# Decoder kernel, state-space stage: scans issued in pairs, once per two groups

## The chip, the cores and the metric

One core of one Trainium2 chip runs the whole program. The metric is the device time of one execution in microseconds; lower is better. The engines are TensorE (PE; its weight loads are listed apart as PEld), VectorE (DVE), ScalarE (ACT), GpSimd (POOL) and SyncE (SP), each with a queue of its own that it works through in order.

## What is computed

Six blocks with residual additions over x of 4 x 256 tokens of 256 elements: self-attention, an expert layer chosen by token number, a mixture of experts, a state-space block (stage D of the kernel), an attention over given keys and values (stage E), and another mixture of experts (stage F). The change touches only the state-space block. Its core is this, for each batch and chunk of 128 tokens:

```python
Lm = jnp.exp(segsum(A))                       # 64 heads x 128 x 128, zero above the diagonal
Y_diag = jnp.einsum('bcshn,bczhn,bhcsz,bczhp->bcshp', Cm, Bm, Lm, X)
states = jnp.einsum('bcshn,bhcs,bcshp->bchpn', Bm, decay_states, X)
...
Y_off = jnp.einsum('bcshn,bchpn,bhcs->bcshp', Cm, states, state_decay_out)
return (Y_diag + Y_off).reshape(b, l, h, p)
```

## The kernel before

A planner, `schedule`, writes one list of steps, and every engine walks through the same list and issues its own part of each step, so the list sets the order on each queue. Between engines stand semaphores.

In stage D the work is cut into 8 units (4 batches x 2 chunks of 128 tokens), numbered u = 0 to 7, and each unit into 16 groups of 4 heads, numbered hg = 0 to 15. Over all units the groups are k = 16u + hg, 0 to 127. A step `("ssd", "D", (u, hg))` does for its group k:

- PE: two bf16 matmuls of 512 columns into one bank of a ring of three (`a_bank`): the mask of later tokens (line 1450), then the decay exponents (line 1452), which has 15 rows of contraction. Then `scan` of group k - 3 (`LAG = 3`, line 95).
- ACT: the exponential from that bank into tile M[k % 4] (line 1055). Before it, ACT waits until the scan of group k - 4 has read that tile.
- DVE: M[k % 4] times the products C·B of the group (line 1807), in place.

`scan` (line 1114) is four fp32 matmuls, one per head, each with a stationary tile of 32 columns of its own and 128 columns of M. Each shows in the trace as two MATMUL rows, so one scan is 8. It waits for the multiplication on DVE of the same group. The four write the four quarters of the partitions of one bank, O; four groups in a row accumulate into one block of 128 columns of it.

Behind each `ssd` step the planner places other work of the stage (`beside`): projections of a later batch (`din`: PE line 1391, then ACT lines 983 and 985, DVE line 1749, ACT line 996, DVE line 1759) at groups 1, 4 and 9 of units 0 to 4; of the next unit: `at` (PE 1418) at group 6, `dz` (PE 1397) at 8, `zs` (ACT, DVE 1767) at 10, `xt` (PE 1428) at 12, `cb` (PE 1437, DVE 1797) at 13; of the last unit: `y_t` at 3 (ACT line 1066 copies the finished bank O, PE line 1260 turns it, DVE lines 1833 to 1839 finish it), `dy_t` (PE 1484, ACT 1071) at 5 and `dy` (PE 1490) at 7; of this unit, at group 0, `state` (PE 1466 in even units, PE 1476 and DVE 1816 in odd ones). After units 2, 4 and 6 DVE also normalises a batch for stage E. Within a step, PE issues the two decay matmuls, then the scan, then the work beside it.

Of the kernel before, what the change touches and what calls it, by code (L numbers as in the profile page):

```python
# [78 lines left out]
NHG = NV // HG  # L79
# [15 lines left out]
LAG = 3  # L95
# [272 lines left out]
def decoder(nc, A, out, stages="ABCDEF"):  # L368
    steps = schedule(stages)
    at = number(steps)  # L370
    with ExitStack() as ctx:
# [702 lines left out]
        def _(pe):  # L1074
# [27 lines left out]
            def scan(s, u, hg):  # L1102

                k = NHG * u + hg
                if hg == 0:
                    bk = o_bank("ssd", s, u)

                    pe.wait_ge(xsp_ready, u + 1)
                pe.wait_ge(m_ready, k + 1)
                bk = O[at["O"]["ssd", s, u] % 2]  # L1110
                quarter, h = divmod(hg, HG)
                for j in range(HG):

                    ins = mm(bk[j * 32:(j + 1) * 32, quarter * P:(quarter + 1) * P],  # L1114
                             xsp[u % 2][:, quarter, h, j, :, :].rearrange("p q w -> p (q w)"),
                             M[:, k % NM, j * P:(j + 1) * P], start=(h == 0), stop=(h == HG - 1), skip_group_check=True)
                ins.then_inc(m_used, 1)

            pe.wait_ge(const_in, 64)
            for kind, s, i in steps:  # L1120
# [28 lines left out]
                elif kind == "qkv_mm" and s == "A":  # L1149
                    i, t = i  # L1150
# [42 lines left out]
                elif kind == "m_t":  # L1193
                    k = attn_index(s, i)
# [6 lines left out]
                elif kind == "pv":  # L1201
                    i, step = i
# [177 lines left out]
                elif kind == "din":  # L1380
                    b, j = i
                    if PAIRS * b + j < beside_c:
                        pe.wait_ge(mix_in, 96)
                        bk, full = t_bank("din", s, b, j), t_full
                    else:
                        bk, full = a_bank("din", s, b, j), a_full
                    pe.wait_ge(t_read, at["T"]["lt", s, b] + 1)
                    for h in range(2):
                        ct = 2 * j + h
                        for k in range(KD):  # L1390
                            ins = mm(bk[:, h * L:(h + 1) * L], win[:, k, ct * P:(ct + 1) * P],  # L1391
                                     xnT_of(s)[:, k, b * L:(b + 1) * L], start=(k == 0), stop=(k == KD - 1))
                    ins.then_inc(full, 1)
                elif kind == "dz":
                    bk = v_bank("dz", s, i)
                    for k in range(KD):
                        ins = mm(bk[:, :], xnT_of(s)[:, k, i * P:(i + 1) * P], win[:, k, CONV:CONV + DI],  # L1397
                                 start=(k == 0), stop=(k == KD - 1))
                    ins.then_inc(v_full, 1)
                elif kind == "dt_in":  # L1400
                    bk = t_bank("dt_in", s, i)
                    pe.wait_ge(t_read, at["T"]["lt", s, B - 1] + 1)
                    for u in range(NU):
                        for k in range(KD):
                            ins = mm(bk[:, u * NV:(u + 1) * NV], xnT_of(s)[:, k, u * P:(u + 1) * P],
                                     win[:, k, CONV + DI:], start=(k == 0), stop=(k == KD - 1))
                    ins.then_inc(t_full, 1)
                elif kind == "acum":

                    pe.wait_ge(dt_ready, 1)  # L1410
                    for k in range(2):
                        bk = t_bank("acum", s, k)
                        mm(bk[:, :], tri[:, k, :], t_max, start=True, stop=True).then_inc(t_full, 1)
                elif kind == "at":
                    bk = t_bank("at", s, i)
                    pe.wait_ge(ap_ready, 1)
                    for h in range(2):
                        ins = tr(bk[:, :].bitcast(BF16)[0:RA, h * P:(h + 1) * P],
                                 ap_[:, i, 2 * h:2 * h + 2, :, :].rearrange("p j m g -> p (j m g)"), identb[:, :])
                    ins.then_inc(t_full, 1)  # L1420
                elif kind == "xt":
                    b, c = divmod(i, NT)

                    pe.wait_ge(xs_ready, (CT // 2) * (b + 1))
                    for part in range(2 if c == 0 else 1):
                        bk = a_bank("xt", s, i, part)
                        for k in range(4):
                            ins = tr(bk[:, k * P:(k + 1) * P], xs[:, b % 2, 4 * part + k, c * P:(c + 1) * P], ident[:, :])
                        ins.then_inc(a_full, 1)
                elif kind == "cb":  # L1430
                    b, c = divmod(i, NT)

                    banks = [v_bank("cb", s, i, par) for par in range(2)]
                    for g2_ in range(NG // 2):
                        for par in range(2):
                            rows = slice(NS * par, NS * par + NS)
                            ins = mm(banks[par][:, g2_ * P:(g2_ + 1) * P], xs[rows, b % 2, 4 + g2_, c * P:(c + 1) * P],
                                     xs[rows, b % 2, 8 + g2_, c * P:(c + 1) * P], start=True, stop=True)
                            if g2_ == NG // 2 - 1:
                                ins.then_inc(v_full, 1)  # L1440
                elif kind == "ssd":
                    u, hg = i
                    if hg == 0:

                        if u == 0:
                            pe.wait_ge(hot_in, 64)
                        pe.wait_ge(rows_landed, 16 * 6 * (u + 1))
                    bk = a_bank("ssd", s, u, hg)

                    mm(bk[:, :], identb[:, :], maskt[:, :].unsqueeze(1).to_broadcast([P, HG, P]),  # L1450
                       start=True, stop=False, skip_group_check=True)
                    mm(bk[:, :], rows_z[u % 2][:, hg, :], rows_s[u % 2][:, :, hg, :], start=False, stop=True,  # L1452
                       skip_group_check=True).then_inc(a_full, 1)
                    k = NHG * u + hg - LAG
                    if k >= 0:
                        scan(s, *divmod(k, NHG))
                elif kind == "ssd_end":
                    for k in range(NHG * i - LAG, NHG * i):
                        scan(s, *divmod(k, NHG))
                elif kind == "state" and i % 2 == 0:  # L1460
                    bk = t_bank("state", s, i)
                    pe.wait_ge(xd_ready, i // 2 + 1)
                    pe.wait_ge(a_read, at["A"]["xt", s, i, 1] + 1)
                    for g_ in range(NG):
                        lo = NS * (g_ % 2)
                        ins = mm(bk[lo:lo + NS, (g_ // 2) * NS:(g_ // 2 + 1) * NS], Bt[:, g_ * NS:(g_ + 1) * NS],
                                 XD[:, g_ * NS:(g_ + 1) * NS], start=True, stop=True)
                    ins.then_inc(t_full, 1)
                elif kind == "state":
                    b = i // NT  # L1470
                    pe.wait_ge(t_read, at["T"]["state", s, i - 1] + 1)
                    banks = [v_bank("state", s, i, par) for par in range(2)]
                    for g2_ in range(NG // 2):
                        for par in range(2):
                            rows = slice(NS * par, NS * par + NS)
                            ins = mm(banks[par][:, g2_ * NS:(g2_ + 1) * NS], xs[rows, b % 2, 8 + g2_, P:L],
                                     stt[rows, g2_, :], start=True, stop=True)
                            if g2_ == NG // 2 - 1:
                                ins.then_inc(v_full, 1)
                elif kind == "dy_t":  # L1480
                    bk = t_bank("dy_t", s, i)
                    pe.wait_ge(yf_ready, i + 1)
                    for k in range(DI // P):
                        ins = tr(bk[:, k * P:(k + 1) * P], yf[:, k * P:(k + 1) * P], ident[:, :])
                    ins.then_inc(t_full, 1)
                elif kind == "dy":
                    bk = v_bank("dy", s, i)
                    pe.wait_ge(t_read, at["T"]["dy_t", s, i] + 1)
                    for k in range(DI // P):
                        ins = mm(bk[:, 0:D], yfT[:, k, :], wout[:, k, :], start=(k == 0), stop=(k == DI // P - 1))  # L1490
                    ins.then_inc(v_full, 1)
# [434 lines left out]
```

## Time and profile before

| what | value |
|---|---|
| median of 3 runs | 1000.64 us |
| lowest and highest | 997.29 and 1004.06 us |
| span of the profiled execution | 1004.2 us |
| of it, state-space groups (first decay matmul to last scan) | about 461 to 713 us |
| PE busy over the span | 822.1 us (82%) |
| DVE busy over the span | 584.5 us (58%) |

The span is counted from the first to the last instruction of the profiled execution. No separate time was taken for that execution; its span lies at the upper end of the three runs. In the rows, times are microseconds from the start of the span. "idle before <-X" in brackets is how long the engine stood idle before that row and what released it.

### The profile page before, as it was taken

How to read it: one execution, taken by the hardware profiler on the slowest of the kernel's cores; microseconds unless marked ns; L12 is line 12 of the kernel's file. 1: busy time of each engine (PE TensorE's matmuls, PEld its weight loads, DVE VectorE, ACT ScalarE, POOL GpSimd, SP SyncE). 2: the span in 40 equal slices, each digit the busy share in tenths (PEclk: the TensorE clock that was granted, in tenths of full speed). 3: DMA queues.
4: the chain of work that ended last, by engine and by line, in shares of the span. 5: the costliest groups of instructions: out<-in, count | busy, mean ns of one | idle time of the engine just before them, and what ended most of it. 6: DMA issues, size and time to landing. Idle time of an engine off the chain costs nothing.

```text
span 1004.2 us, 14716 instructions
## 1 busy us (share of the span) xinstructions
PE 822.1 (82%) x5680; PEld 530.7 (53%) x5680; DVE 584.5 (58%) x1184; ACT 380.8 (38%) x653; POOL 221.1 (22%) x210
## 2 busy tenths in 40 slices
PE   1678777599899799657899899999757777899998
PEld 0334443258677588523444444434434554677776
DVE  5765642544545457535787878547577663645443
ACT  1124334001444356244455445335213345444442
POOL 3200000123433322041110111001231111432432
PEclk9989878599899899866999999669578799799999
DMA  8000001000121211100000000000000001232231
GB/s 307 28 2 1 3 1 48 1 0 23 57 79 55 72 48 32 18 0 5 5 6 5 4 3 5 5 5 2 1 2 2 2 2 49 64 93 64 79 92 45
DMA packets 17669, 32.98 MB, mean 33 GB/s; under 512 B 5642, under 2 KB 9610, under 8 KB 17320
## 3 DMA queue, kind: packets, MB, share of 16 engines
q1 hardware_dynamic: 17600, 32.03, 10.4%
q8 instruction: 46, 0.75, 0.3%
q14 instruction: 23, 0.19, 0.1%
HBM read 30.06 MB, written 1.05 MB: 31 GB/s over the span
## 4 chain that ended last, share of the span: by engine, by line
PE 57%; DVE 21%; issue 11%; ACT 5%; POOL 4%; DMA 1%; SPq 0%; DVEq 0%; ACTq 0%; POOLq 0%
PE bank L1352 12%; PE bank L1376 8%; PE bank L1391 5%; PE bank L1299 3%; PE bank L1114 3%; PE bank L1452 2%; DVE s_arena L1807 2%; DVE s_xn L1523 2%; PE bank L1490 2%; PE bank L1314 2%; PE bank L1450 2%; DVE s_arena L1749 2%; PE bank L1243 2%; DVE s_arena L1595 2%; PE bank L1397 2%
## 5 line engine op out<-in xcount | busy, mean ns | idle before, releaser
L777 POOL TENSOR_TENSOR s_wl<-s_wmoe,s_wh 128x768 fp32r<-128x768 f32 x54 | 99.3, 1841 | 174.2 <-ACT s_wh L947 174.2
L1807 DVE TENSOR_TENSOR s_arena<-s_arena 128x512 f32<-128x512 f32 x128 | 89.8, 711 | 54.9 <-ACT s_arena L1055 54.5
L1055 ACT ACTIVATE s_arena<-bank 128x512 f32<-128x512 f32 x128 | 74.6, 602 | 74.8 <-PE bank L1452 74.8
L896 ACT ACTIVATE s_arena<-bank 128x512 f32<-128x512 f32 x96 | 56.6, 597 | 106.9 <-PE bank L1219 59.2
L1595 DVE TENSOR_REDUCE s_arena<-bank 128x2 f32<-128x512 f32 (+1 forms) x96 | 64.8, 687 | 35.0 <-PE bank L1190 18.6
L1714 DVE TENSOR_TENSOR s_act<-bank,s_sg_moe 128x512 f32<-128x512 f32 x54 | 37.4, 692 | 81.5 <-PE bank L1352 75.0
L1352 PE MATMUL bank<-s_xh,s_wh 128*128 128x512 f32 x216 | 73.2, 421 | 8.0 <-POOL s_wl L777 7.9
L959 ACT CAST s_ah<-s_act 128x512 fp32r<-128x512 f32 x54 | 33.6, 622 | 101.8 <-DVE s_act L1719 79.1
L1352 PE MATMUL bank<-s_xl,s_wh 128*128 128x512 f32 x216 | 69.4, 403 | 0.0
L1352 PE MATMUL bank<-s_xh,s_wl 128*128 128x512 f32 x216 | 69.2, 403 | 0.0
L1376 PE MATMUL bank<-s_wh,s_ah 128*128 128x256 f32 x216 | 66.5, 308 | 2.8 <-DVE s_al L1725 2.8
L1749 DVE SCALAR_TENSOR_TENSOR s_arena<-s_arena,s_convw 128x256 f32<-128x256 f32 x144 | 68.0, 513 | 0.6
L1376 PE MATMUL bank<-s_wl,s_ah 128*128 128x256 f32 x216 | 61.5, 285 | 0.0
L1376 PE MATMUL bank<-s_wh,s_al 128*128 128x256 f32 x216 | 61.5, 285 | 0.0
L1725 DVE TENSOR_TENSOR s_al<-s_act,s_ah 128x512 fp32r<-128x512 f32 x54 | 37.4, 692 | 40.3 <-ACT s_ah L959 40.2
L725 POOL TENSOR_TENSOR s_rstd<-s_ve,s_mhalf 128x2 f32<-128x2 f32 x24 | 16.6, 692 | 192.2 <-DVE s_ve L1515 192.1
L1450 PE MATMUL bank<-s_maskt,s_identb 128*128 128x512 bf16 x128 | 53.5, 418 | 5.5 <-issue 5.5
L1391 PE MATMUL bank<-s_xnT,s_win 128*128 128x256 f32 x192 | 53.5, 428 | 0.0
L1376 PEld LDWEIGHTS bank<-s_wh,s_ah 128*128 128x128 f32 x216 | 41.5, 192 | 13.4 <-issue 8.2
L1146 PE MATMUL bank<-s_ident,s_xn 128*128 128x128 f32 x80 | 15.7, 330 | 38.9 <-DVE s_xn L1523 36.7
L1352 PEld LDWEIGHTS bank<-s_xl,s_wh 128*128 128x128 f32 x216 | 42.3, 196 | 9.8
L1352 PEld LDWEIGHTS bank<-s_xh,s_wh 128*128 128x128 f32 x216 | 39.3, 198 | 15.5 <-DVE s_act L1714 7.0
(220 smaller groups left out, 1673.5 us busy)
## 6 DMA issues: line engine op xcount, KB each, us to landing
s_wmoe<-in_wF SPq DMA_DIRECT2D x28, 384.0 KB, 3.1
s_wmoe<-in_wC SPq DMA_DIRECT2D x26, 384.0 KB, 3.1
s_win<-in_win SPq DMA_DIRECT2D x1, 2112.0 KB, 10.5
s_x<-in_x SPq DMA_DIRECT2D x4, 256.0 KB, 3.5
s_early<-in_ctxT SPq DMA_DIRECT2D x1, 1024.0 KB, 9.5
s_ctxn<-in_ctx SPq DMA_DIRECT2D x1, 1024.0 KB, 12.4
out_x<-s_x SPq DMA_DIRECT2D x4, 256.0 KB, 2.9
s_xnT<-in_tok SPq DMA_DIRECT2D x1, 512.0 KB, 7.8
```

Source lines behind the costliest of these rows:

```text
L777: g.tensor_tensor(wl[:, w % NS_, :], wmoe[:, w % NW, :], wh[:, w % NS_, :], ALU.subtract).then_inc(wl_ready, 1)
L896: a.activation(PT[:, p % NPT, :], AR[n % 3][:, :], ACT.Exp).then_inc(a_read, 1)
L1055: a.activation(M[:, k % NM, :], AR[n % 3][:, :], ACT.Exp).then_inc(a_read, 1)
L1352: ins = mm(G[2 * (n % 2) + half][:, :], a_[:, k, half, :], b_[:, k, toks], start=(p_ == 0), stop=(p_ == len(parts) - 1))
L1376: ins = mm(Y[t // NT][:, (t % NT) * D:(t % NT + 1) * D], a_[:, w % NA, t * P:(t + 1) * P], b_[:, w % NS_, 2 * KD * P:], start=(j == 0 and ...
L1391: ins = mm(bk[:, h * L:(h + 1) * L], win[:, k, ct * P:(ct + 1) * P], xnT_of(s)[:, k, b * L:(b + 1) * L], start=(k == 0), stop=(k == KD - 1))
L1450: mm(bk[:, :], identb[:, :], maskt[:, :].unsqueeze(1).to_broadcast([P, HG, P]), start=True, stop=False, skip_group_check=True)
L1595: v.tensor_reduce(nM[:, q, h0:h0 + heads], V[n % 2][:, :].rearrange("p (h k) -> p h k", h=heads), AX.X, ALU.max, negate=True).then_inc(v_r ...
L1714: v.tensor_tensor(act_[:, w % 2, :], G[2 * (n % 2) + 1][:, :], sg_moe[:, n % 2, :], ALU.mult).then_inc(g_read, 1)
L1725: v.tensor_tensor(al[:, w % NA, :], act_[:, w % 2, :], ah[:, w % NA, :], ALU.subtract).then_inc(al_ready, 1)
L1749: ins = v.scalar_tensor_tensor(o, raw[:, m % NRAW, h, KS - 1 - k:KS - 1 - k + L], convw[:, ct, KS - 1 - k:KS - k], o, ALU.mult, ALU.add)
L1807: v.tensor_tensor(m, m, CBs[:, u % 2, hg // (NV // NG):NG:NG // HG, :], ALU.mult).then_inc(m_ready, 1)
```

## The change

PE no longer issues one scan in every group. In odd groups it issues two, of groups k - 3 and k - 2; in even groups it issues none. After the last unit two scans are left over instead of three. The order of all other instructions, the semaphores and the tiles stay as they are. The line below that reads `range(NHG * i + 1 - LAG, NHG * i)` is the rest after the last unit.

```diff
@@ -1451,11 +1451,12 @@
                        start=True, stop=False, skip_group_check=True)
                     mm(bk[:, :], rows_z[u % 2][:, hg, :], rows_s[u % 2][:, :, hg, :], start=False, stop=True,
                        skip_group_check=True).then_inc(a_full, 1)
-                    k = NHG * u + hg - LAG
-                    if k >= 0:
-                        scan(s, *divmod(k, NHG))
+                    if hg % 2:
+                        for k in range(NHG * u + hg - LAG, NHG * u + hg - LAG + 2):
+                            if k >= 0:
+                                scan(s, *divmod(k, NHG))
                 elif kind == "ssd_end":
-                    for k in range(NHG * i - LAG, NHG * i):
+                    for k in range(NHG * i + 1 - LAG, NHG * i):
                         scan(s, *divmod(k, NHG))
```

## Rows read from the trace of the kernel before

**Rows 1.** The page: busy time of each engine, and the chain that ended last
```profile
PE 822.1 (82%) x5680; PEld 530.7 (53%) x5680; DVE 584.5 (58%) x1184; ACT 380.8 (38%) x653; POOL 221.1 (22%) x210
PE 57%; DVE 21%; issue 11%; ACT 5%; POOL 4%; DMA 1%; SPq 0%; DVEq 0%; ACTq 0%; POOLq 0%
```

**Rows 2.** Busy time by stretch, the whole stage; columns in the first line
```profile
core 0: us, PE busy (x) PEld busy (x) DVE busy (x) ACT busy (x) POOL busy (x), PEclk, DMA share, GB/s
461.00:713.00 252.00, 233.66 (x1830) 112.89 (x1833) 183.00 (x356) 122.42 (x237) 30.41 (x45) 0.88 0.02 4
```

**Rows 3.** Timeline of PE, one group of unit 3: start, duration
```profile
581.50 0.39 PE L1450 MATMUL bank<-s_maskt,s_identb 128*128 128x512 bf16 x1
...
582.13 0.43 PE L1114 MATMUL bank<-s_arena,s_wmoe 128*32 128x128 f32 x8
582.49 0.39 PE L1450 MATMUL bank<-s_maskt,s_identb 128*128 128x512 bf16 x1
```

**Rows 4.** Timeline of PE in the first attention, same matmul form
```profile
95.43 0.42 PE L1243 MATMUL bank<-s_arena 128*32 128x128 f32 x8
95.79 0.66 PE L1277 MATMUL bank<-s_ident,s_arena 128*128 128x128 f32 x4
...
116.67 0.64 PE L1243 MATMUL bank<-s_arena 128*32 128x128 f32 x16
117.24 0.33 PE L1146 MATMUL bank<-s_ident,s_xn 128*128 128x128 f32 x1
...
144.91 1.08 PE L1243 MATMUL bank<-s_arena 128*32 128x128 f32 x16
145.92 0.61 PE L1186 MATMUL bank<-s_masks,s_identb 128*128 128x512 bf16 x1
```

**Rows 5.** Timeline of PE, unit 0, step 2, which has no scan
```profile
468.22 0.60 PE L1452 MATMUL bank<-s_arena 15*128 15x512 bf16 x1
468.75 0.52 PE L1450 MATMUL bank<-s_maskt,s_identb 128*128 128x512 bf16 x1
```

**Rows 6.** Timeline of PE in unit 2: `at` of the next unit
```profile
537.76 0.31 PE L1418 MATMUL bank<-s_identb,s_arena 128*96 128x128 bf16 x2 [0.20 <-ACT s_arena L1071]
```

**Rows 7.** Timeline of DVE and PE, end of unit 3
```profile
588.55 1.56 DVE L1807 TENSOR_TENSOR s_arena<-s_arena 128x512 f32<-128x512 f32 x1
590.16 0.42 PE L1114 MATMUL bank<-s_arena,s_wmoe 128*32 128x128 f32 x8 [0.97 <-DVE s_arena L1807]
```

**Rows 8.** Timeline of all engines, from unit 1 into unit 2
```profile
524.47 0.42 PE L1114 MATMUL bank<-s_arena,s_wmoe 128*32 128x128 f32 x8 [0.96 <-DVE s_arena L1807]
...
526.27 0.42 PE L1114 MATMUL bank<-s_arena,s_wmoe 128*32 128x128 f32 x8
526.63 1.99 PE L1391 MATMUL bank<-s_xnT,s_win 128*128 128x256 f32 x8
526.74 1.88 DVE L1807 TENSOR_TENSOR s_arena<-s_arena 128x512 f32<-128x512 f32 x3
...
531.01 0.61 ACT L1066 COPY s_arena<-bank 128x512 f32<-128x512 f32 x1
...
531.76 0.63 PE L1260 MATMUL bank<-s_ident,s_arena 128*128 128x128 f32 x4 [1.26 <-ACT s_arena L1066]
```

**Rows 9.** Timeline of ACT, from unit 2 into unit 3
```profile
562.83 1.02 ACT L983 ACTIVATE s_arena<-bank,s_convw 128x256 f32<-128x256 f32 x2 [3.84 <-DVE s_arena L1816]
```

**Rows 10.** Timeline of PE and DVE, unit 5, step 3
```profile
629.06 0.65 PE L1114 MATMUL bank<-s_arena,s_wmoe 128*32 128x128 f32 x8 [0.76 <-DVE s_arena L1807]
629.64 1.11 PE L1260 MATMUL bank<-s_ident,s_arena 128*128 128x128 f32 x4
629.88 1.89 DVE L1807 TENSOR_TENSOR s_arena<-s_arena 128x512 f32<-128x512 f32 x3
```

**Rows 11.** Timeline of PE, unit 6, step 3
```profile
659.79 0.72 PE L1260 MATMUL bank<-s_ident,s_arena 128*128 128x128 f32 x4 [0.90 <-ACT s_arena L1066]
```

**Rows 12.** Busy time by stretch, around two unit boundaries; columns as in rows 2
```profile
523.70:527.10 3.40, 2.51 (x36) 1.50 (x37) 3.40 (x6) 2.34 (x5) 0.17 (x1) 1.00 0.01 2
...
591.90:595.30 3.40, 3.35 (x15) 2.42 (x16) 2.41 (x4) 0.57 (x1) 0.00 (x0) 0.50 0.00 0
```

## The prediction

> **What bounds the kernel now.** I read the page first: PE is busy 82% of the span and carries 57% of the chain that ended last, DVE 21% [rows 1]. Then the busy times of the stage alone: PE is busy 233.66 of 252 us, so only about 18 us of it are PE idle, and DVE is busy 183 [rows 2]. That looks like a stage bound by PE, but a mean hides what the timeline shows. Each of units 0 to 4 has two parts. In its first part (groups 3 to 9) PE runs nearly without a gap. Behind the projection of group 9 the chain goes over to ACT and DVE: DVE works without a stop through the multiplications of groups 10 to 13 and the convolution and gating pieces between them, the last one stretched to 1.56 us, and PE, which had run ahead, stands 0.97 us at the scan of group 13 [rows 7]; one batch earlier it is 0.96 [rows 8]. I call this part the wall. PE time saved inside it is only waited away. After the wall the chain goes by the projection of group 1 of the next unit, through ACT's queue to its copy of the finished bank, and back to PE's turn of it, for which PE stands 1.26 us [rows 8]. Units 5 to 7 have no projections and are mostly PE, apart from the normalisations on DVE.
>
> **What the pair saves.** In a run of groups with nothing beside them, a scan starts at 582.13 and the next mask matmul at 582.49: a scan alone costs PE 0.36 us [rows 3]. The kernel has no two scans back to back, save in the very end where DVE paces them. The nearest rows are the value matmuls of the attention, of the same form (32 stationary columns, 128 x 128 fp32): eight of them cost 95.79 - 95.43 = 0.36, sixteen 117.24 - 116.67 = 0.57 [rows 4]. Twice 0.36 less 0.57 gives 0.14 to 0.15 a pair; I take 0.14. At half clock sixteen cost 1.01 [rows 4] and eight 0.58 [rows 10], so 0.15 or 0.16 a pair. In PE busy terms a pair can save between 0 (if the wait of the second scan breaks it off) and 0.15; I take the row's value, since a scan is the same form, and since a wait that is already met costs nothing visible where the mask matmul, which has one too, follows a scan. What could eat it is the new neighbour: in even groups the decay matmul (15 rows) is now followed at once by a full-width one. Step 2 of unit 0, which has no scan, shows that neighbour [rows 5]: 0.53 from start to start at half clock, which is what 512 columns and a little take, so nothing new is paid. There are 64 pairs: 64 x 0.14 = 9 us at the most, if every one came through.
>
> The Trainium skill (TensorEngine Tiling, Key Properties) says that changing the tiling mode drains TensorE. By that rule a pair has one change fewer than two single scans, and the rows of the attention agree in size; it says nothing of what the change does to waits.
>
> **What comes through, unit by unit.** Scans of even groups keep their place. Those of odd groups move one step earlier, ahead of the work beside the odd step and of the next decay matmuls, and need their multiplication on DVE that much sooner.
>
> First part, units 1 to 4. Between PE's turn (line 1260, group 3) and the projection of group 9 there were six scans, 6 x 0.36 = 2.13 with unrounded 0.355; now there are three pairs, 3 x 0.57 = 1.72. That is 0.41 less, the odd first scan having moved into PE's wait of 1.26 ahead of line 1260. Of it 0.14 is lost again: the `at` matmul behind groups 5 and 6 already stands 0.20 for an ACT copy that hangs on the projection of group 4 [rows 6]. So -0.27 a unit, -1.1 for four. Unit 0 has seven scans before the wall, 2.49, and now four pairs, 2.28: -0.2.
>
> The wall: four of the eight pairs (in steps 11, 13, 15 and 1) lie in it or behind it, gain 0.
>
> Behind the wall, unit 1 into 2. Now the scan of group 13 stands directly behind that of group 12 and waits for the same release, at 524.47. Before, the decay matmuls of the next group were issued ahead of it, and filled part of that wait; now they stand behind it, 0.36 + 0.62 for scan and `state` matmuls, 0.63 for one more decay pair: scan 14 comes at about 526.7 instead of 526.27. Then scan 15 must also be done before the projection may start. Its multiplication is the first of the three that start at 526.74 [rows 8], about 0.68 long, so it ends at 527.42 and the scan starts at 527.48. The projection starts at 527.84 instead of 526.63: +1.21. Queued behind it is all of ACT's work for that projection, ACT's copy (531.01) and PE's turn (531.76) [rows 8], so the +1.21 reaches the chain. Unit 3 into 4 repeats the pattern, by the same working +0.97. Unit 0 into 1 is an even unit, where the next decay pair fits into another wait of PE's; there only the second scan of the pair comes ahead of the projection, 1.01 - 0.58 = +0.43 at the half clock it has there. Unit 2 into 3: ACT stands 3.84 us for the DVE of the normalisation [rows 9], so a projection 0.4 later costs 0. Unit 4 into 5 has no projection: 0. Together +2.6.
>
> Unit 5. At step 3 the scan of group 0 starts at 629.06 and the turn follows at 629.64. Now scan 1 stands between them, and its multiplication starts only at 629.88 [rows 10], ends near 630.56; scan 1 then takes 0.58, and the turn starts at about 631.2, +1.57, of which 0.59 is given back since the same scan is gone from step 4: +0.98. Then seven pairs up to step 1 of unit 6, 2 x 0.16 and 5 x 0.14: -1.0.
>
> Unit 6. Scan 1 moves into a wait of 0.90 ahead of the turn [rows 11]: -0.59 at half clock, and five pairs before the last decay matmul of the unit, 3 x 0.16 + 2 x 0.14: -0.75. Unit 7: DVE binds at both ends; one pair counts, -0.1. The very last scans follow DVE's multiplications as before: 0.
>
> Sum: -1.1 - 0.2 + 2.6 + 1.0 - 1.0 - 1.35 - 0.1 = -0.15, which is nothing. The M ring costs nothing: ACT waits for the scan four groups back, which comes in the same step as before for even groups and one step earlier for odd ones. POOL, SP and the DMAs of `at` keep their order. They wait for scans only through the count of used tiles, which is no later than before except by the waits named.
>
> **The clock.** At the exit of unit 3 the granted clock goes to 0.50 (1.2 GHz) for 3.4 us, right after PE stood 0.97 us; at the exit of unit 1, after almost the same wait, it stays at 1.00 (2.4 GHz) [rows 12, 7, 8]. The longer waits of the new order (about 1.7 us at group 13 in place of 0.97) may bring such a stretch at the exit of unit 1 too; it costs up to half of 3.4, 1.7 us. I add 0.5 to 1 for this. The profiled execution (1004.2) lies at the upper end of the three runs; taken against the median 1000.64 the forecast is 1001.3 us.
>
> **The rivals.**
> - A, forecast: savings in the PE-bound parts and waits behind the walls cancel. 1001.3, own range 997 to 1005. For it: the waits at the exits and in unit 5 [rows 8, 10], whose waits don't depend on how PE is fed. Chance 0.62.
> - B, faster: the waits behind the wall are absorbed (the multiplication of group 15 comes earlier, or ACT has slack that I don't see), and the PE parts gain all. At the most 64 x 0.14 = 9: 992; with only the PE-bound pairs (about 28) and the scans moved into waits, 5: 996. Against it: DVE has no gap in the wall. Chance 0.14.
> - C, slower: the clock. Every longer stand of PE at a scan of an odd group (exits of units 1 and 3, step 3 of unit 5, the end of unit 7) is followed by one more half-clock stretch, 4 x 1.7 = 7 on top of A: 1008. It decides when more than one of these places shows 0.50 where it showed 1.00, so that it outweighs the 4 us that pairs and moved scans give. For it: the stretch after the 0.97 wait. Against: the exit of unit 1. Chance 0.16.
> - D, the pair doesn't pay: the second scan costs the full 0.36 behind the first. Then some 28 pairs lose 0.14 each, +4 on A: 1005. Against it: the sixteen rows in 0.57 [rows 4]. Chance 0.08.
>
> **How the numbers follow.** A and parts of B and D lie within a few us of no change; the three runs of the kernel before lie up to 3.4 us from their median, so a measurement of this kernel can hardly tell less than 1% (10 us) from no change. The range reaches from just inside B's far end of 992 to just above C's 1008: 993 to 1009. Faster by over 1% needs all of B and luck with the clock, 0.03; slower by over 1% is the upper part of C, 0.06; within 1%, 0.91.
>
> **What would show it.** In the profile after: sixteen rows of line 1114 in a block, 0.57 to 0.58 from its start to the next matmul (D: 0.71). Between lines 1260 and the projection of group 9 about 0.3 to 0.4 us less per unit. At the exits of units 1 and 3 a wait at scan 13 of about 1.7 us and one at scan 15 of some 0.5, with the projection of group 1 about 1 us later against the scan of group 13 (B: no such delay). In unit 5 a wait of about 1.3 us between scans 0 and 1. PE busy of the stage falls by less than 9 us, its idle rises by nearly as much, and the stage's 252 us stay within 2 at the same clock. The prediction is wrong if the granted clock of the stage moves far from 0.88, or if DVE's wall itself changes length, which no row here suggests.

## The result and the profile after

The changed kernel takes 1009.22 us (median of 10 runs, 1006.32 to 1011.51); the kernel before takes 1002.01 in its 10 runs beside it. The ratio is 1.0071 with a 95% interval of 1.0049 to 1.0093: slower, by about 7 us. The profiled execution of the changed kernel took 1006.76 us (span 1005.0), one of its faster ones, while that of the kernel before (span 1004.2) was one of its slower ones. The two spans differ by 0.8 us and can't show the 7 us by themselves; what differs inside them can.

The page after, busy times and chain, as in [rows 1]:

```profile
PE 815.9 (81%) x5680; PEld 536.7 (53%) x5680; DVE 584.1 (58%) x1184; ACT 380.9 (38%) x653; POOL 221.6 (22%) x210
PE 57%; DVE 22%; issue 11%; ACT 6%; POOL 3%; DMA 1%; SPq 0%; DVEq 0%; ACTq 0%; POOLq 0%
```

PE is busy for 6 us less, and no share of the chain moves by more than a point. The timeline of PE, unit 4, the pair ahead of the projection of group 9 (start, duration):

```profile
613.64 0.65 PE L1114 MATMUL bank<-s_arena 128*32 128x128 f32 x16
614.21 0.48 PE L1391 MATMUL bank<-s_xnT,s_win 128*128 128x256 f32 x1
```

The pair costs 0.57 (614.21 - 613.64), as [rows 4] had it. The exit of unit 1 into unit 2, all engines, which answers to [rows 8]:

```profile
519.76 0.43 PE L1114 MATMUL bank<-s_arena,s_wmoe 128*32 128x128 f32 x8 [1.52 <-DVE s_arena L1808]
...
522.01 0.43 PE L1114 MATMUL bank<-s_arena,s_wmoe 128*32 128x128 f32 x8
522.03 1.88 DVE L1808 TENSOR_TENSOR s_arena<-s_arena 128x512 f32<-128x512 f32 x3
...
522.76 0.42 PE L1114 MATMUL bank<-s_arena,s_wmoe 128*32 128x128 f32 x8 [0.32 <-DVE s_arena L1808]
523.12 1.99 PE L1391 MATMUL bank<-s_xnT,s_win 128*128 128x256 f32 x8
...
528.25 0.63 PE L1260 MATMUL bank<-s_ident,s_arena 128*128 128x128 f32 x4 [1.40 <-ACT s_arena L1066]
```

From scan 13 to the projection it is now 523.12 - 519.76 = 3.36, before 526.63 - 524.47 = 2.16 [rows 8]: +1.20. And unit 5, step 3, which answers to [rows 10]:

```profile
631.47 0.44 PE L1114 MATMUL bank<-s_arena,s_wmoe 128*32 128x128 f32 x8 [1.45 <-DVE s_arena L1808]
633.03 0.66 PE L1114 MATMUL bank<-s_arena,s_wmoe 128*32 128x128 f32 x8 [1.12 <-DVE s_arena L1808]
633.62 1.12 PE L1260 MATMUL bank<-s_ident,s_arena 128*128 128x128 f32 x4
```

From scan 0 to the turn 2.15 in place of 0.58: +1.57. All of this is where the prediction put it. What isn't shows in the wall of unit 2:

```profile
549.20 0.43 PE L1114 MATMUL bank<-s_arena 128*32 128x128 f32 x8 [0.65 <-DVE s_arena L1808]
549.56 1.86 PE L1437 MATMUL bank<-s_arena 64*128 64x128 f32 x16
551.36 0.61 PE L1450 MATMUL bank<-s_maskt,s_identb 128*128 128x512 bf16 x1
...
553.50 1.08 PE L1114 MATMUL bank<-s_arena 128*32 128x128 f32 x16
```

PE stands 0.65 us at scan 11, the second of the pair in step 13, and right behind it the matmuls take 1.6 to 1.8 times as long: the mask 0.61 where it took 0.39 of row time, the pair 1.02 from start to start where it took 0.57. For the next 13.70 us PE is busy all the time and DVE for 10.43: the end of this wall is no longer set by DVE but by PE, and late. Busy times by stretch, the columns as in [rows 2], the first line for the whole stage, then the stretch with the stand in it, the one behind it, four more at the lower clock, and all that follows the stage:

```profile
456.30:710.60 254.30, 231.57 (x1834) 119.56 (x1834) 182.99 (x356) 122.30 (x237) 30.84 (x45) 0.87 0.02 4
546.40:549.80 3.40, 2.63 (x28) 1.25 (x29) 3.34 (x7) 2.50 (x6) 1.34 (x3) 1.00 0.00 0
549.80:563.50 13.70, 13.70 (x81) 7.79 (x79) 10.43 (x27) 3.01 (x6) 2.98 (x4) 0.50 0.01 1
529.40:532.80 3.40, 3.40 (x9) 2.62 (x9) 3.33 (x7) 0.60 (x1) 0.00 (x0) 0.50 0.00 0
566.90:570.30 3.40, 3.40 (x10) 1.98 (x8) 3.37 (x8) 0.60 (x1) 0.00 (x0) 0.50 0.00 0
631.80:645.40 13.60, 12.48 (x70) 6.55 (x67) 6.53 (x14) 3.52 (x7) 0.00 (x0) 0.50 0.02 5
686.40:693.20 6.80, 6.80 (x39) 2.79 (x31) 3.68 (x6) 2.17 (x4) 0.00 (x0) 0.50 0.01 2
710.60:1005.00 294.40, 243.19 (x1846) 180.72 (x1846) 154.32 (x319) 112.58 (x175) 82.38 (x64) 0.88 0.14 42
```

The reader should see that PE is at the lower of its two clock levels (0.50, 1.2 GHz) for 13.7 us in unit 2, behind a stand at an odd scan; at 529.4 and 566.9 behind the wait for ACT's copy ahead of the turn; and in unit 7 behind the wait of scan 1. The stretch at 631.8, around the waits of unit 5, isn't new: the kernel before has one there too, and a second long one in unit 6 that the changed kernel doesn't have (lines of the kernel before):

```profile
626.10:643.10 17.00, 16.24 (x82) 6.75 (x81) 9.15 (x25) 5.30 (x10) 0.69 (x1) 0.50 0.03 7
660.20:677.30 17.10, 17.10 (x72) 6.80 (x69) 5.92 (x10) 4.22 (x8) 0.00 (x0) 0.50 0.03 6
```

At the exit of unit 1 of the changed kernel, behind a stand of 1.52, the clock stays at the upper level. Who waited for whom, PE's longest waits on DVE's multiplication in stage D (us in total, times, longest), first after, then before:

```profile
PE bank L1114 <- DVE s_arena L1808: 13.6, 15, 3.0
```

```profile
PE bank L1114 <- DVE s_arena L1807: 6.7, 8, 1.9
```

### The profile page after: what moved, and what is told of

It is laid out like the page before. It is cut to its first block, busy times and chain, and to the rows that moved or that the text cites. A ratio compares the mean times of both kernels' runs of the same rounds, so it can differ in the third digit from the quotient of the medians.

```text
span 1005.0 us, 14716 instructions
## 1 busy us (share of the span) xinstructions
PE 815.9 (81%) x5680; PEld 536.7 (53%) x5680; DVE 584.1 (58%) x1184; ACT 380.9 (38%) x653; POOL 221.6 (22%) x210
## 4 chain that ended last, share of the span: by engine, by line
PE 57%; DVE 22%; issue 11%; ACT 6%; POOL 3%; DMA 1%; SPq 0%; DVEq 0%; ACTq 0%; POOLq 0%
PE bank L1352 13%; PE bank L1376 8%; PE bank L1391 5%; PE bank L1299 3%; PE bank L1114 2%; DVE s_xn L1524 2%; DVE s_arena L1808 2%; PE bank L1452 2%; PE bank L1314 2%; PE bank L1450 2%; PE bank L1491 2%; DVE s_arena L1596 2%; PE bank L1243 2%; DVE s_arena L1750 2%; POOL s_rstd L725 1%
## 5 line engine op out<-in xcount | busy, mean ns | idle before, releaser
L1391 PE MATMUL bank<-s_xnT,s_win 128*128 128x256 f32 x192 | 56.5, 445 | 0.0
L1376 PEld LDWEIGHTS bank<-s_wh,s_ah 128*128 128x128 f32 x216 | 41.5, 192 | 13.5 <-issue 8.2
L1352 PEld LDWEIGHTS bank<-s_xh,s_wl 128*128 128x128 f32 x216 | 42.4, 196 | 10.0
```

Source lines behind the costliest of these rows:

```text
L1352: ins = mm(G[2 * (n % 2) + half][:, :], a_[:, k, half, :], b_[:, k, toks], start=(p_ == 0), stop=(p_ == len(parts) - 1))
L1376: ins = mm(Y[t // NT][:, (t % NT) * D:(t % NT + 1) * D], a_[:, w % NA, t * P:(t + 1) * P], b_[:, w % NS_, 2 * KD * P:], start=(j == 0 and ...
```

## The experiments

One number is used throughout: the **half-clock time** of a run, 2 x (1 - its mean granted clock) x its span, since the clock has two levels; given as the mean over those timed runs of a kernel that its ratio counts. The lower level is half of the upper one, so half-clock time by itself costs at most half of its length. In the table, "before" is the kernel before on the same chip in the same session. "The fill" means that PE repeats the mask matmul of a coming group into its bank before it is due: the values are the same, and the aim is that PE works where it would stand. The first repeat waits for the bank to be free, as the mask matmul itself would later on (once, for 0.6 us, in the trace of the changed kernel filled in all units).

| kernel | median, us | before, us | ratio [95%] | half-clock time / of before |
|---|---|---|---|---|
| before, again | 998.97 | 998.67 | 0.9999 [0.9973, 1.0025] | 204 / 205 |
| changed, again | 1009.14 | 1003.03 | 1.0071 [1.0048, 1.0095] | 234 / 211 |
| pairs at 1, 3, 11, 13, 15 | 1014.61 | 998.67 | 1.0157 [1.0122, 1.0192] | 238 / 205 |
| pairs at 5, 7, 9 | 1002.47 | 1000.16 | 1.0025 [0.9988, 1.0062] | 221 / 210 |
| pairs in unit 7 | 1008.76 | 1000.16 | 1.0049 [1.0006, 1.0092] | 218 / 210 |
| pairs in units 0 to 4 | 1011.05 | 1003.03 | 1.0091 [1.0060, 1.0122] | 235 / 211 |
| pairs trailing 4 and 3 | 1011.27 | 1000.16 | 1.0092 [1.0064, 1.0121] | 240 / 210 |
| changed, filled in units 0 to 4 | 1003.77 | 998.67 | 1.0045 [1.0027, 1.0064] | 208 / 205 |
| changed, filled in all | 993.42 | 1003.03 | 0.9910 [0.9876, 0.9945] | 185 / 211 |
| before, filled in units 0 to 4 | 1003.04 | 1000.16 | 1.0004 [0.9970, 1.0037] | 210 / 210 |
| before, filled in all | 994.15 | 1004.62 | 0.9914 [0.9882, 0.9947] | 187 / 216 |
| trailing 4 and 3, filled in all | 991.00 | 1003.03 | 0.9894 [0.9851, 0.9938] | 196 / 211 |

Three theories stood against each other. C: the order costs about nothing, as summed, and the 7 us are half-clock time behind PE's stands. W: the waits themselves cost more than summed. N: any reordering of PE would have cost this. Each kernel was timed beside the kernel before, whose median moved between 998.7 and 1004.6 from one session to the next, so kernels are compared by their ratios.

**The two kernels once more.** No edit.

> The kernel before, unchanged, once more, for a second profile and the granted clock of each of its runs. Theory C (clock): the 7 us between the kernels are half-clock time, so the runs of this one show a mean clock above that of the changed kernel (0.879 to 0.895, middle 0.886) or as much PE-bound time less at half clock, and its stage D needs about as long as that of the changed kernel once half-clock stretches are taken out. Theory W (waits): the clock is the same and its stage D is some 7 us shorter at full clock. Time: within 0.3% of the kernel before.

> The changed kernel once more, for a second profile and for times on the same chip as the filled ones. 6 to 8 us above the kernel before, half-clock time 20 to 28 us above it.

The changed kernel repeats its ratio and has 23 us more half-clock time. Its stage D takes 254.3 us in the first profile and 253.8 in the second. That of the kernel before repeats less well: 252.6 in the first profile, 245.5 in this one:

```profile
460.60:706.10 245.50, 226.71 (x1834) 110.73 (x1834) 182.86 (x356) 122.28 (x237) 30.41 (x45) 0.91 0.02 4
```

The difference is one place. The first profile has a half-clock stretch of 17 us in unit 6, the second has none; the others are the same but for the one at the end of the stage, which starts where unit 7 then is. W expected a stage that is 7 us shorter at the same clock. It is 8 us shorter, but at 0.91, not 0.87, so W isn't borne out.

How far the clock goes with the time can be read in pieces. The table has the time from the turn in step 3 of one unit (first matmul of `y_t`) to the turn in the next, the last row to the one behind the last unit, and, in brackets, how much of it was at half clock, read from the trace:

| stretch | before, second profile | changed, first profile | difference |
|---|---|---|---|
| unit 1 to 2 | 31.51 (0) | 32.44 (0) | +0.93 |
| unit 2 to 3 | 34.17 (3.4) | 38.26 (17.1) | +4.09 |
| unit 3 to 4 | 33.14 (3.4) | 35.23 (6.8) | +2.09 |
| unit 4 to 5 | 30.60 (3.5) | 31.88 (5.3) | +1.28 |
| unit 5 to 6 | 30.16 (13.5) | 28.20 (11.8) | -1.96 |
| unit 6 to 7 | 24.67 (0) | 24.79 (0.2) | +0.12 |
| unit 7 to the end | 22.67 (9.4) | 24.75 (14.5) | +2.08 |

The second profile of the changed kernel gives the same to 0.02 us. In the first one of the kernel before, unit 6 to 7 takes 31.86 with 17.1 at half clock; the other pieces are the same to 0.02. The two largest losses stand in pieces where the half-clock time grows; what the order alone does to each piece is read further down, with the fill.

**Where the pairs stand.** A counter holds the next scan, and each step issues scans up to a limit:

```diff
-                    k = NHG * u + hg - LAG
-                    if k >= 0:
-                        scan(s, *divmod(k, NHG))
+                    last = NHG * u + hg - (2 if hg in (1, 3, 11, 13, 15) else LAG)
+                    while scanned[0] <= last:
+                        scan(s, *divmod(scanned[0], NHG))
+                        scanned[0] += 1
```

The other three have `hg in (5, 7, 9)`, `hg % 2 and u == 7` and `hg % 2 and u < 5` in that place.

> Pairs only at steps 1, 3, 11, 13 and 15 of each unit, where the second scan has to wait for its multiplication on DVE; single scans trailing by 3 elsewhere. Keeps all the added stands of PE, gives up the pairs at 5, 7 and 9. Theories C and W: nearly all of the loss is back, 1006 to 1010. Theory N (any reordering of PE costs the same, wherever it is): about half of it or less in proportion to the steps, no clear answer between 1003 and 1008; with the result of pairs trailing by 4 and 3 it is decided.

> Pairs only at steps 5, 7 and 9 of each unit, where every multiplication is done long before; single scans trailing by 3 elsewhere. No stand of PE gets longer. Saving: none in units 0 to 4 beyond 0.1 each, since seven scans in place of six now come ahead of the projection of group 9 and the at matmul waits for ACT anyway; 3 x 0.14 in each of units 5 to 7: about 1.5 us. Theory C (half-clock time behind PE's longer stands): 996 to 1000 where the kernel before has 999, half-clock time as in the kernel before (205 us a run). Theory N (any reordering): 2 to 4 us slower.

> Pairs as in the change, but in unit 7 alone; units 0 to 6 as in the kernel before. In unit 7 PE stands longer at scans 1 and 9. Static sum: nothing, DVE sets the end there. Theory C: half-clock time around the end of the stage and behind it grows by 10 to 20 us, time 3 to 5 us above the kernel before: a good half of the loss comes from here. Against it: within 1 us of the kernel before, and the loss sits in units 0 to 5.

> Pairs as in the change in units 0 to 4, single scans trailing by 3 in units 5 to 7: the complement of the kernel with pairs in unit 7 alone, less unit 5's wait between scans 0 and 1. If the loss adds up by places: 1 to 4 us slower than the kernel before, half-clock time up by some 10 us. If unit 7's stand were the whole of the loss: same as the kernel before.

Pairs where the second scan has to wait cost 1.6%, more than all pairs together and above what any theory gave (1006 to 1010 by C and W, less by N; 1014.61 measured). Pairs where nothing waits cost 0.25%, with an interval that holds no change. That is inside what N expected of them (2 to 4 us), though the interval reaches C's forecast too; their half-clock time is 11 us up (some 6 without the slowest of the six runs), where C had none. But a reordering doesn't cost the same wherever it is, as N had it. The places don't add up either: pairs in units 0 to 4 alone cost 0.9% (1 to 4 us were expected, a miss), those in unit 7 alone 0.5%, all of them 0.7%. The trace of the kernel with pairs in units 0 to 4 shows one reason: up to unit 4 its pieces are those of the changed kernel (38.24 from unit 2 to 3, 17.1 of it at half clock), behind that those of the kernel before with the long stretch of unit 6 (31.86, 17.1 at half clock), which neither profile of the changed kernel has (24.8). Half-clock time goes up in each. In unit 7 the timeline of PE shows the step from one to the other, of the kernel with pairs there only:

```profile
690.42 0.43 PE L1114 MATMUL bank<-s_arena,s_wmoe 128*32 128x128 f32 x8 [1.14 <-DVE s_arena L1809]
...
692.54 0.94 PE L1114 MATMUL bank<-s_arena,s_wmoe 128*32 128x128 f32 x16
693.40 1.12 PE L1486 MATMUL bank<-s_ident,s_arena 128*128 128x128 f32 x4
694.31 0.63 PE L1451 MATMUL bank<-s_maskt,s_identb 128*128 128x512 bf16 x1
```

Scan 1 waits 1.14, and 2 us later the pair's last matmuls, the turn of line 1486 and the mask are at half clock, to 699.5. The kernel before has no such stretch in unit 7's first half.

**Pairs that need nothing earlier.** Even steps issue the pair of groups k - 4 and k - 3, with five M tiles. The fifth doesn't fit into the region by itself (it has 27200 columns, and 27404 were needed, so that version has no time), so the small tile `stt` moves to unused words of another buffer:

```diff
-        NM = 4
+        NM = 5
...
-        stt = cut(NG // 2 * NS).rearrange("p (g n) -> p g n", g=NG // 2)
+        stt = wmoe[:, :, :].rearrange("p n w -> p (n w)")[:, XS:XS + NG // 2 * NS].rearrange("p (g n) -> p g n", g=NG // 2)
...
+                    last = NHG * u + hg - (LAG if hg % 2 == 0 else LAG + 1)
```

> Pairs in even groups, of groups k-4 and k-3, with five M tiles instead of four (the small tile stt moves to unused words of another buffer to make room). No scan needs its multiplication earlier than before; the pairs save 0.14 each. Theory C: half-clock time at or below that of the kernel before (205 us), time 4 to 6 us below it, 993 to 995 where that has 999. Theory N: about 7 us slower than the kernel before. If the pairs themselves lower the clock: half-clock time near the 229 us of the changed kernel although no stand is longer, and no gain.

This is the miss that teaches most: C had 4 to 6 us faster. PE's waits on DVE at the scans are no longer than before (6.3 us in all, before 6.7), and still it is 0.9% slower with the most half-clock time of all, 240 us. Total, times and longest in stage D, the first two lines of this kernel, the last of the kernel before:

```profile
PE bank L1261 <- ACT s_arena L1066: 10.4, 6, 4.1
PE bank L1114 <- DVE s_arena L1809: 6.3, 7, 1.8
```

```profile
PE bank L1260 <- ACT s_arena L1066: 7.5, 6, 2.0
```

And its stage D by busy times:

```profile
461.00:719.40 258.40, 236.60 (x1834) 122.79 (x1833) 182.88 (x356) 123.01 (x237) 29.98 (x45) 0.84 0.02 4
```

So longer stands at odd scans aren't needed for the loss. What this kernel shares with the changed one is more standing time of PE in all: the waits that the views of stage D list for PE, without the one at its start, add up to 18.1 us before, 21.8 in the changed kernel and 21.9 here, 10.4 of it ahead of the turn. That pairs save PE work where DVE or ACT sets the pace, and that the saving comes back as such stands, is the reading that fits; no run shows it by itself.

**The fill.** If the loss is the clock, more work for PE should make all of them faster. The first edit, of the changed kernel (a line for step 13 and one for the turn are left out here):

```diff
+            def fill(s, u, hg, n):
+                for _ in range(n):
+                    mm(a_bank("ssd", s, u, hg)[:, :], identb[:, :], maskt[:, :].unsqueeze(1).to_broadcast([P, HG, P]),
+                       start=True, stop=False, skip_group_check=True)
...
+                    if hg == 15 and u < 5:
+                        fill(s, u + 1, 0, 6 if u % 2 else 2)
```

> The changed kernel with PE's stands filled: the mask matmul of the next group is issued up to 6 times in advance into its bank (0.22 us each at full clock): 6 or 2 ahead of the scans of step 15, 2 ahead of those of step 13 in even units, 5 ahead of the turn in step 3. The repeated matmuls write the same values, the output is unchanged. Same waits and order otherwise. Theory C: fewer half-clock stretches follow the stands, so with more work it is 3 to 6 us faster than the changed kernel, 1003 to 1006. Theory W: same as the changed kernel or up to 2 us slower, 1009 to 1011.

> The changed kernel with the stands filled as in the first filled one (up to 6 repeated mask matmuls at steps 15, 13 and 3 of units 0 to 4), and also ahead of the scans of step 3 in units 5 (8 of them) and 7 (6), and of step 11 in unit 7 (8). Values unchanged. Theory C (half-clock time behind PE's stands): half-clock time down to that of the kernel before or below it, and the time within 2 us of the kernel before, 3 us or more under the changed kernel. Theory W (the waits themselves): no better than the changed kernel.

> The kernel before with its own stands of PE filled by repeated mask matmuls of the next group (values unchanged): 4 or 2 behind the scan of step 15, 5 ahead of the turn in step 3, units 0 to 4. Theory C: the half-clock stretches of 3.4 us at the exits of units 0, 2 and 3 are gone from the profile; of each up to 1.7 us comes back where PE sets the end, so 2 to 4 us faster than the kernel before, with 5 to 10 us less half-clock time. Against C: no change of the half-clock time, time equal or 1 to 2 us worse by the added work.

> The kernel before with all of its longer stands filled, as the changed one had them when it came out 9 to 10 us faster than before: 4 or 2 repeated mask matmuls in step 15 of units 0 to 4, 5 ahead of the turn in units 1 to 4, 4 and 3 in units 6 and 7, 3 ahead of scan 0 in unit 5, 8 ahead of scan 9 in unit 7. Values unchanged. Theory C: half-clock time 20 to 25 us under the kernel before, time 5 to 9 us under it; then the pairs themselves are worth the small rest, 1 to 4 us, as the sum of the prediction has it. If pairs and fill only work together: within 2 us of the kernel before.

> Pairs trailing by 4 and 3 with five M tiles (which came out 9 us slower, with 30 us more half-clock time), with its stands filled by repeated mask matmuls: 4 or 2 in step 15 of units 0 to 4, 5 ahead of every turn in step 3, 6 ahead of the scans of step 12 in unit 7. If the loss of the unfilled one is PE work that the pairs save, comes back as stands and lowers the clock: 5 us or more better than that, near the kernel before (0 to 4 us faster than it). If the loss has another cause (the order itself, the fifth tile): still 7 to 10 us slower than the kernel before.

With 66 more matmuls, the changed kernel filled in all units is 9 to 10 us faster than the kernel before, where it was expected to come within 2 us of it, and some 16 faster than unfilled. Its stage D, again by the busy times of the stretch:

```profile
461.00:698.00 237.00, 223.87 (x1900) 113.32 (x1899) 182.36 (x356) 121.71 (x237) 30.83 (x45) 0.98 0.02 4
```

254.3 us at a clock of 0.87 have become 237.0 at 0.98. The same was done to the kernel before at its own stands, with 52 matmuls, as a control: 0.9914, with its stage at

```profile
461.10:702.80 241.70, 230.71 (x1886) 112.36 (x1885) 182.82 (x356) 122.22 (x237) 30.41 (x45) 0.95 0.02 4
```

and to the pairs trailing by 4 and 3 with 55, from 1.0092 down to 0.9894, the fastest of all at 991.00 us, though its interval overlaps those of the other two filled kernels. The fifth tile and the moved `stt` are the same in both, so neither by itself makes this order slower than the kernel before:

```profile
459.70:694.50 234.80, 224.52 (x1889) 116.21 (x1888) 182.51 (x356) 122.52 (x238) 29.96 (x45) 0.94 0.02 4
```

Where the fill counts can be read too. In units 0 to 4 alone it does nothing for the time of the kernel before (a miss; 2 to 4 us were expected): of the three short stretches only the one at the exit of unit 3 is gone, which takes unit 3 to 4 from 33.14 us to 31.51, while those at the exits of units 0 and 2 are still there. It takes 0.26% off the changed one, where the two intervals overlap. There units 1 to 5 run at full clock and in the same times as with the fill in all units, but the profile has 13.7 us of half clock around the turn of unit 7 (677.6 to 691.3), where the unfilled one has 6.8. The rest comes with the fill in units 5 to 7.

With the clock near the upper level in both, the order itself can be read, again from turn to turn, both filled in all units:

| stretch | before, filled | changed, filled | difference | predicted |
|---|---|---|---|---|
| unit 1 to 2 | 31.52 | 32.44 | +0.92 | -0.27 + 1.21 |
| unit 2 to 3 | 34.17 | 33.89 | -0.28 | -0.27 |
| unit 3 to 4 | 31.52 | 32.44 | +0.92 | -0.27 + 0.97 |
| unit 4 to 5 | 30.45 | 31.65 | +1.20 | -0.27 + 1.57 |
| unit 6 to the end | 47.35 | 46.60 | -0.75 | -1.35 - 0.1 |

From unit 5 to 6 the filled kernel before takes 28.60 us, 6.8 of it at half clock, and the filled changed one 23.13 with none: even with half of 6.8 taken off, the order saves 2 us there, where 0.59 + 1.0 was predicted. In the second row it has 3.4 us of half clock, and the difference is still the predicted one, so no cost of them shows. Together with the 2 us the rows give about zero for the order, unit 0 not counted.

Beside the table of the unfilled kernels this parts the two causes. From unit 1 to 2, with the clock up throughout, the order costs +0.9 filled and unfilled, so the fill by itself changes nothing there. From unit 2 to 3 the order gives -0.28, but unfilled the changed kernel was 4.09 slower, with 13.7 us more of half clock; from unit 6 to the end the order gives -0.75, and unfilled it was +2.20, with 5.3 us more.

## Why the prediction was wrong

The step that failed is "The clock": "I add 0.5 to 1 for this". About 7 us is what is left for this term when the order's own sum comes out near zero, and it belonged in the forecast, not at a chance of 0.16. Half-clock time is 23 us above that of the kernel before, which can hold up to 11.5 us, and with the stands filled in both kernels no difference is left between them (0.9910 and 0.9914, each to about 0.0033).

The rest, by its own steps. **What the pair saves**: right for a pair that isn't broken by a wait, 0.57, and rival D is out; a second scan that has to wait costs its full 0.36 behind the wait (549.20 to 549.56), as the step allowed. By the Trainium skill (TensorEngine Tiling, Key Properties) a change of tiling mode drains TensorE. The row agrees, with 0.14 less for a pair than for two single scans; that size is the row's and not the rule's. **What comes through, unit by unit**: right to a few tenths in four stretches of five, by the table above; units 6 and 7 gave half of what was put down, and unit 6, for which 1.35 was put down, gave nothing at full clock (24.68 and 24.71 us to the turn of unit 7); units 5 to 6 gave more. The sum "-0.15, which is nothing" stands, in part since these two errors cancel; the times of the two filled kernels agree with it to some 3 us. But the scans of group 11 (the second of the pair in step 13), whose wait of 0.65 in units 0, 2 and 4 the prediction doesn't name, mattered through what came behind them. **A** fell with the clock term. **B** is out: the delays behind the wall are there in full. **C** had the kind of cause, and its size, 1008 against 1009.2, was luck: at none of its four places (exits of units 1 and 3, step 3 of unit 5, end of unit 7) is there a stretch at 0.50 that wasn't there before. The exit of unit 1 stays at 1.00, and the other three had one already. The new ones lie behind the turn (529.4 and 566.9), behind the scans of group 11 in units 2 and 4, and at scan 1 of unit 7, and the longest, 13.7 us in unit 2, came behind a stand that no rival named. Its condition was wrong as well, since the kernel whose pairs trail by 4 and 3 waits no longer at its scans and lost the same. The range's upper end, 1009.0, was 0.2 short; the chance of 0.91 for within 1% holds the result.

The prediction had one stretch after a 0.97 stand and one counterexample [rows 12], and priced a single stretch of 3.4 us. What it didn't do was to add up how long the clock was low, from 2 x (1 - clock) x length: 61 of the stage's 252 us in that profile, 44 in the next one of the same kernel. A term that moves by 17 us between two profiles of one program is not a half-microsecond correction. The signs that the prediction gave can't show the error either: against the first profile of the kernel before, stage D is only 1.7 us longer (254.3 for 252.6) at 0.87 for 0.88. That profile had the long stretch of unit 6, and one profile alone doesn't tell that the same kernel can run without it.

**What stays open.** Why the clock falls at one stand and not at another, and why one low stretch lasts 3.4 us and another 13.7 or 17, was not tried apart. The scan of group 11 stands 0.65 us in units 0, 2 and 4 of the changed kernel, and behind it the clock stays up, is low for 13.7 us, and is low for 3.4, the same in both profiles. Nor is it shown how the loss divides between stage D and what follows it: the stretch behind the stage, where nothing was changed, takes 294.4 and 294.5 us at 0.88 in the two profiles of the changed kernel, and 290.7 and 292.4 at 0.90 in those of the kernel before; but the filled kernel that is 9 us faster also has 294.5 there. The fill changes when things start as well as how busy PE is; that it did the same to three different orders, and left the one piece without half clock as it was, speaks for the clock, and no run separates the two further.

## What to carry to other kernels

When a change takes work off PE in a stretch that another engine sets, the saved time can come back as standing time, and behind standing time PE can run at half clock for longer than it stood: add up the half-clock time of the profile, per unit, before a change is called neutral. Take more than one profile of the kernel before, since one half-clock stretch more or less can outweigh the change, as it did here (252.6 and 245.5 us for the same stage). Where PE stands for a microsecond or so in a stage that is otherwise PE-bound, try harmless repeats of a matmul there; here they were worth 0.9% to the kernel before and 1.6% to the changed one, while no reordering without them was faster than the kernel before. Try them in all units: in some alone they did little.

## What the runs showed that I had not expected

PE's clock fell to 0.50 for 13.7 us behind a stand of only 0.65 us, though it didn't behind each of that length, and more work, placed in all units, made all three orders faster: 66 added matmuls took the changed kernel from 1.0071 to 0.9910. The Trainium skill (TensorE: Matmul & The Clock Gate, Part 1: The HAM clock gate) says that the clock is gated by how busy PE has recently been; the fill agrees, with a stage clock of 0.98 in place of 0.87. And a program whose times spread over 10 us, as the kernel before does, can do so by a single stretch that is there or not, 17 us at half clock in unit 6, while the changed kernel's two profiles agree to 0.02 us from turn to turn. That the other runs differ for the same reason isn't shown, since only one of a set has a profile, but their clocks fit: beside the second profile, every run of the kernel before above 1003 us has a mean clock of 0.888 to 0.891, and every one under 999 us has 0.896 to 0.904.
